# The experts' products in three single passes of numbers in parts, with x held by halves of the tokens

## What is computed

```python
# attention, 16 heads of 32; no scaling of the scores
xq, xk, xv = x @ wq.T, x @ wk.T, x @ wv.T
probs = softmax(einsum('bqhd,bkhd->bhqk', xq, xk))
x = layernorm(x + einsum('bhqk,bkhd->bqhd', probs, xv) @ wo.T)
# experts: E = 8, rank R = 64, one chosen per token
logits = x @ Wr.T + br
expert_weight, expert_idx = max and argmax of softmax(logits)
h = einsum('nd,erd->ner', x, A)
y = einsum('ner,eor->neo', h, B) / 64
x = layernorm(x + y[chosen expert] * expert_weight)
```

## Time and profile before

| | |
|---|---|
| runs | 1540.71 us median of 3 (1540.62 to 1541.03) |
| profiled execution | 1541.77 us, of which 1540.0 us from the first to the last instruction (its span) |
| mean granted clock of PE | 0.986 of full speed |
| busy | PE 1480.7 us (96%), POOL 1159.7 (75%), DVE 932.6 (61%), ACT 776.8 (50%) |
| opening, before slot 0 | 55.9 us |
| slots 0 to 7 | 311.1 us |
| slots 8 and 9 | 43.9 and 45.2 us |
| slots 10 to 14 | 242.6 us |
| slots 15, 16 and 17 | 44.1, 42.4 and 46.3 us |
| slots 18 to 22 | 235.7 us |
| slots 23, 24 and 25 | 44.0, 41.8 and 44.8 us |
| slots 26 to 30 | 205.1 us |
| slot 31 and closing | 33.8 and 103.3 us |
| DMA | 153.13 MB, the queues' packets take 33.5% of the 16 engines' span |

### The profile page before, as it was taken

How to read it: one execution, slowest core, us unless ns; L and a number is a source line. 1 busy time by engine, 2 the same in 40 slices (tenths; PEclk the granted TensorE clock), 3 DMA queues, 4 the chain that set the end, 5 groups by cost and what they waited for, 6 DMA issues and landing times.

```text
span 1540.0 us, 20530 instructions
## 1 busy us (share of the span) xinstructions
PE 1480.7 (96%) x6872; PEld 865.1 (56%) x6872; DVE 932.6 (61%) x1722; ACT 776.8 (50%) x1421; POOL 1159.7 (75%) x654
## 2 busy tenths in 40 slices
PE   7999999989999999999999999999999999999998
PEld 5755456655645656556645555556664555554354
DVE  6756667655565566665566556666556666564633
ACT  3455555544555455545546445554555545455232
POOL 0376879978798867877889987777987888888301
PEclk9999999999999999999999999999999999899999
DMA  7355624444431422427242323324514222210001
GB/s 237 92 165 150 208 80 135 142 148 131 124 77 42 117 84 61 126 80 254 52 130 64 90 70 103 104 68 153 158 39 148 49 49 63 56 42 29 1 13 42
DMA packets 80217, 153.13 MB, mean 99 GB/s; under 512 B 19041, under 2 KB 26225, under 8 KB 79729
## 3 DMA queue, kind: packets, MB, share of 16 engines
q1 hardware_dynamic: 78720, 150.24, 33.5%
q0 software_dynamic: 336, 1.07, 0.2%
q10 hardware_dynamic: 1056, 0.52, 0.1%
HBM read 102.52 MB, written 48.49 MB: 98 GB/s over the span
## 4 chain that ended last, share of the span: by engine, by line
PE 78%; issue 7%; DVE 6%; POOL 4%; DMA 3%; ACT 1%; SPq 1%; POOLq 0%; ACTq 0%; DVEq 0%
PE w L684 14%; PE pv L827 13%; PE mx L805 13%; PE sc L815 13%; PE w L750 6%; PE w L763 6%; PE w L719 5%; DVE mxc L1037 3%; PE mx L778 2%; POOL Psum L595 2%; DMA spread_s<-den_s 1%; PE mx L743 1%; PE mx L763 1%; PE w L727 1%; DMA den_parts<-spread_s 1%
## 5 line engine op out<-in xcount | busy, mean ns | idle before, releaser
L1037 DVE TENSOR_REDUCE mxc<-mx 128x1 f32<-128x512 f32 x1024 | 683.8, 686 | 463.9 <-PE mx L805 460.8
L908 ACT ACTIVATE P<-sc 128x512 f32<-128x512 f32 x1024 | 598.8, 597 | 504.8 <-PE sc L815 490.6
L595 POOL TENSOR_TENSOR Psum<-Psum,P 128x1024 f32<-128x1024 f32 x296 | 695.7, 2383 | 26.5 <-ACT P L908 24.7
L815 PE MATMUL sc<-stack 98*128 98x512 f32 x1024 | 540.4, 530 | 7.5 <-ACT P L908 6.9
L805 PE MATMUL mx<-stack 96*128 96x512 f32 x1024 | 407.1, 402 | 9.1 <-DVE mxc L1037 4.6
L815 PEld LDWEIGHTS sc<-stack 98*128 98x128 f32 x1024 | 194.3, 190 | 142.7 <-issue 81.0
L805 PEld LDWEIGHTS mx<-stack 96*128 96x128 f32 x1024 | 195.9, 191 | 124.2 <-issue 70.8
L827 PE MATMUL pv<-P,V 128*32 128x512 f32 x2048 | 250.4, 607 | 0.0
L592 POOL TENSOR_TENSOR Psum<-P 128x1024 f32<-128x1024 f32 x50 | 118.6, 2390 | 132.7 <-ACT P L908 126.4
L684 PE MATMUL w<-xT_s,wqk_s 128*128 128x512 f32 x624 | 197.9, 408 | 12.0 <-DVE xT_s L1054 10.4
L684 PEld LDWEIGHTS w<-xT_s,wqk_s 128*128 128x128 f32 x624 | 116.9, 192 | 67.7 <-issue 43.4
(11 more groups left out here) (147 smaller groups left out, 1086.8 us busy)
## 6 DMA issues: line engine op xcount, KB each, us to landing
stack<-qk_parts SPq DMA_DIRECT2D x186, 256.0 KB, 4.3
qk_parts<-split SPq DMA_DIRECT2D x56, 512.0 KB, 3.4
wqk_s<-wqk_parts SPq DMA_DIRECT2D x24, 512.0 KB, 4.5
xT_s_f<-xT SPq DMA_DIRECT2D x8, 1024.0 KB, 6.5
den_s<-den_parts SPq DMA_DIRECT2D x124, 64.0 KB, 2.1
r_f<-x SPq DMA_DIRECT2D x3, 2048.0 KB, 11.2
out<-r_f SPq DMA_DIRECT2D x12, 512.0 KB, 3.1
qk_parts<-turned SPq DMA_DIRECT2D x8, 512.0 KB, 3.9
```

What stands on the lines that cost most here:

```text
L595: pool.tensor_tensor(sums(s)[:, i, :], sums(s)[:, i, :], P[:, unit % NP, :], ALU.add).then_inc(add_done, 1)
L815: pe.matmul(sc[c][:, :], stack(s, i)[0:KS, 0, 128 * kb:128 * kb + 128], stack(s, i)[0:KS, 1, 512 * c:512 * c + 512], start=True, stop=True ...
L908: act.activation(P[:, unit % NP, 512 * c:512 * c + 512], sc[c][:, :], ACT.Exp).then_inc(exp_done, 1)
L1037: dve.tensor_reduce(mxc[:, q % 2, at:at + 1], BANK["max", g][:, :], AX.X, ALU.max).then_inc(mx_done, 1)
```

## The change

`h`, `z` and `lg` become three single passes of numbers in parts. What follows from that:

- A, B and Wr are split: A and B in slots 4 and 5 by ACT (high) and POOL (low) in r, and kept in DRAM as `a_parts` and `b_parts` of 2 MB each; Wr in slot 2.
- yT and hmT have a high part by ACT as before and a low part by DVE (`yT_low`, `hmT_low`), read from the transpose's bank, which is now free only after that.
- The experts' parts take place: `wide` holds A's parts (or wv's, as before) and a new `wb` holds B's from slot 9 on. x in parts is held for 512 tokens rather than 1024 (`xT_s`; in batches 0 and 1 the second half lies in `wb`). For batches 2 and 3 the pieces of qk are done for the second half of the tokens first, then for the first half; the parts of the second half are kept in DRAM (`keep_x`) and loaded again for `v` (`again_x`) at the start of slots 16 and 24, whose filler starts at half 8. Each slice of the weights is loaded for each piece.
- P has 6 buffers rather than 7, and slots 4 to 7 leave their last two blocks to PE as slots 0 to 3 do.

```diff
-    NP, NMX = 7, 3
+    NP, NMX = 6, 3
...
-    CHUNKS = {"qk": PASSES * KT, "v": PASSES * KT, "o": KT, "part": KT - 1, "h": KT, "z": KT, "t1": 1, "t2": 1, "lg": 1, "den": 1}
-    COST = {"qk": 13, "v": 13, "t1": 24, "t2": 24}
+    CHUNKS = {"qk": PASSES * KT, "v": PASSES * KT, "o": KT, "part": KT - 1, "h": PASSES * KT, "z": PASSES * KT, "t1": 1, "t2": 1,
+              "lg": 1, "den": 1}
+    COST = {"qk": 13, "v": 13, "h": 13, "z": 13, "t1": 24, "t2": 24}
...
-        some = [len(fill) * (n + 1) // (KB + 2) - len(fill) * n // (KB + 2) for n in range(KB + 2)]
+        some = (2, 2, 2, 1, 1, 0, 1, 2, 1, 1) if fill else (0,) * (KB + 2)
...
+            if not final:
+                FROM[at + PAIRS] = 8
...
+            if batch > 1 and turn == 0:
+                KEEP_X[place + 8] = batch
+        if batch > 1:
+            AGAIN_X[HALVES * PAIRS * batch] = batch
+    SPLIT_AT, WR_AT = {"a": HALVES * 4, "b": HALVES * 5 + 8}, HALVES * 2 + 20
...
     def tail(s):
-        return s < 4 or s == LAST
+        return s < PAIRS or s == LAST
...
+        def x_half(b, c):
+            return (wb_f, wb) if b < 2 and c else (xT_f, xT_s)
...
+            def keep_x(b):
+                sp.wait_ge(x_lo, 2 * KT * b + KT)
+                sp.dma_start(x_d[b - 2], xT_s[:, :, :, :].bitcast(f32)).then_inc(x_kept, 16)
+            def again_x(b):
+                sp.wait_ge(qk_ready, 16 * (b + 1))
+                sp.wait_ge(v_ready, KB * b + KB // 2)
+                sp.dma_start(xT_s[:, :, :, :].bitcast(f32), x_d[b - 2]).then_inc(x_again, 16)
...
-                sp.wait_ge(qk_ready, 4 if j < SLICES + 2 else 2 * (j - 1))
+                sp.wait_ge(qk_ready, 4 if j < SLICES + 2 else last_of(j - 2) + 1)
...
-                for s, d in ((a_s, aT), (b_s, bT)):
-                    sp.dma_start(s, d.rearrange("(k p) n -> p k n", p=128)).then_inc(ab_loaded, 16)
+                sp.dma_start(wide[:, :, :, :].bitcast(f32), a_d).then_inc(a_loaded, 16)
+                if b == 1:
+                    sp.wait_ge(qk_ready, 32)
+                    sp.dma_start(wb[:, :, :, :].bitcast(f32), b_d).then_inc(b_loaded, 16)
...
-                    if n % 2 and n >= 17 and n // 2 + 2 < SLICES * B:
-                        load_weights(n // 2 + 2)
+                    if n >= 16 and n == last_of(load_of(n)) and load_of(n) + 2 < LOADS:
+                        load_weights(load_of(n) + 2)
...
+                for n, place in enumerate(SPLIT_AT.values()):
+                    if half == place - 8:
+                        load_raw_ab(n)
+                    if half == place + 24:
+                        store_ab(n)
...
+                for n, place in enumerate(SPLIT_AT.values()):
+                    if half in range(place + 4, place + 4 + 4 * KT, 4):
+                        ab_low(n, (half - place) // 4 - 1)
...
-                for kt in range(KT):
-                    done = pe.matmul(bank[:, 0:E], yT[:, 128 * kt:128 * kt + 128], wr_s[:, kt, :], start=(kt == 0), stop=(kt == KT - 1))
+                for c in range(PASSES * KT):
+                    kt, at = c // PASSES, slice(128 * (c // PASSES), 128 * (c // PASSES) + 128)
+                    done = one_of_three(bank[:, 0:E], [yT[:, i, at] for i in range(2)], [wr_s[:, i, kt, :] for i in range(2)], c)
...
-                done = pe.matmul(bank[:, :], hmT[:, 128 * kt:128 * kt + 128], b_s[:, kt, :], start=(kt == 0), stop=(kt == KT - 1))
+                done = one_of_three(bank[:, :], [hmT[:, i, at] for i in range(2)], [wb[:, i, kt, :] for i in range(2)], c)
...
-                act.activation(yT[:, :], bank[:, :], ACT.Copy).then_inc(yT_done, 1)
+                act.activation(yT[:, 0, :], bank[:, :], ACT.Copy).then_inc(yT_hi, 1)
...
-                act.activation(hmT[:, :], bank[:, :], ACT.Copy, scale=SCALING).then_inc(hmT_done, 1)
+                act.activation(hmT[:, 0, :], bank[:, :], ACT.Copy, scale=SCALING).then_inc(hmT_hi, 1)
...
+            def yT_low(n, bank):
+                dve.wait_ge(yT_hi, n + 1)
+                dve.tensor_tensor(yT[:, 1, :], bank[:, :], yT[:, 0, :].bitcast(f32), ALU.subtract).then_inc(yT_done, 1)
+            def hmT_low(n, bank):
+                dve.wait_ge(hmT_hi, n + 1)
+                dve.scalar_tensor_tensor(out=hmT[:, 1, :], in0=bank[:, :], scalar=SCALING, in1=hmT[:, 0, :].bitcast(f32),
+                                         op0=ALU.mult, op1=ALU.subtract).then_inc(hmT_done, 1)
...
+                    elif kind == "t1":
+                        yT_low(n, bank)
                     elif kind == "lg":
                         largest_logit(n, bank)
                     elif kind == "h":
                         masked(n, bank)
+                    elif kind == "t2":
+                        hmT_low(n, bank)
```

More of the change, by code:

```diff
@@ L208, in build_attention_lora_moe_block @@
         if half in X_PASS:
-            batch, m = X_PASS[half]
-            frees = next_turn(("xi", 2 * KT * batch + m))
+            batch, turn, kt = X_PASS[half]
+            frees = next_turn(("xi", 2 * KT * batch + KT * turn + kt))
         for kind, n, _ in AT.get(half, ()):
@@ L701, in v @@
                 kt, (b, kb) = c // PASSES, divmod(n, KB)
+                half, at = kb // 4, slice(128 * (kb % 4), 128 * (kb % 4) + 128)
+                x_parts = x_half(b, half)[1]
                 if c == 0:
-                    pe.wait_ge(x_lo, 2 * KT * b + KT * (kb // 4 + 1))
+                    if b > 1 and half:
+                        pe.wait_ge(x_again, 16 * (b - 1))
+                    else:
+                        pe.wait_ge(x_lo, 2 * KT * b + KT * (half + 1 if b < 2 else 2))
                     if b > 1:
@@ L707, in v @@
                     pe.wait_ge(wv_lo, kt + 1)
-                done = one_of_three(bank, [xT_s[:, i, kt, 128 * kb:128 * kb + 128] for i in range(2)],
-                                    [wide[:, i, kt, :] for i in range(2)], c)
+                done = one_of_three(bank[:, :], [x_parts[:, i, kt, at] for i in range(2)], [wide[:, i, kt, :] for i in range(2)], c)
                 if c == PASSES * KT - 1:
@@ L1007, in _ @@
                     x_high(*X_HIGH[half])
+                if half == WR_AT:
+                    act.wait_ge(tail_loaded, 32)
+                    act.activation(wr_s[:, 0, :, :], wr_f[:, 1, :, :], ACT.Copy).then_inc(wr_hi, 1)
+                for n, place in enumerate(SPLIT_AT.values()):
+                    if half in range(place, place + 4 * KT, 4):
+                        ab_high(n, (half - place) // 4)
                 for kind, late in (("o", 7), ("z", 11)):
```

212 lines of the change are left out of this document (127 added, 85 removed).

## The result

The changed kernel takes 1638.06 us (median of 4 runs, 1633.08 to 1642.49), the kernel before 1540.87 beside it: a ratio of 1.062, 95% interval 1.058 to 1.066. The forecast was 1551 with a range up to 1567, so the time lies 71 us outside. The sign was the one held likelier; the size was not even near. The profiled execution took 1638.73 us, its span 1636.9.

A forecast was written before the change was run, and what follows sets the result against it. PE, busy 96% of the span, was taken as the bound, with POOL setting slot 7. Terms -4.3 - 13.0 + 14.4 + 4.3 - 6.3 + 5.5 + 3.6 + 6 = +10.2 on 1540.7 gave 1551; own range 1543 to 1560, whole range 1526 to 1567.

The forecast's parts named there:

- The sign: Whole kernel: slower held at 0.55, faster 0.33, same 0.12; said to be decided at 0.6 us for each of 18 places.
- PE, in order, waits 1.3 ... I count 12 such places ... at 1.2 us: +14.4: Slots 10 to 14 and 18 to 22: hmT_low on DVE frees t2's bank late, so PE waits; +14.4 us.
- its twin for slots 26 to 30: Slots 26 to 30: hmT_low delays lg and the maximum, PE waits at six places at 1.8 us; +10.8.
- nothing, as long as that cover stays: After t1: yT_low's later release of the bank costs nothing, the third bank being wanted three halves later with a product between.
- The splits on ACT ... and the opening: nothing: Copies to DRAM, ACT's splits (8 x 0.6) and the opening cost nothing, lying under PE's work.
- I take this 13.3 as gone: Slot 7: its 13.3 us over slot 5 vanish as slots 4 to 7 lose two POOL adds each.
- the splits, forecast at 3.5: Slots 4 to 8: splitting A and B costs 3 us at the dens of slots 4 and 5, 0.5 for a store.
- 3 x 0.7: Closing: the extra VectorE step on yT and hmT is uncovered at the first two and last tile, +2.2 us.
- slot 9: Slot 9: 2.1 MB more of A's and B's parts ahead of the denominators' small transfers makes DVE's reciprocal wait, +5.5 us.
- the waits in slots 15 and 23: The third qk piece needs its own weight slice, which comes 1.8 us late in each slot: +3.6.
- The products' 19.5: Slots 10 to 14, 18 to 22 and 26 to 30: cheaper pieces less dearer lg save 13.0 and 6.5 us.
- the ring does not bind: Rival: DVE is early enough at t2, so the 14.4 and 10.8 vanish; 1526 us, faster; chance 0.2.

The follow-up runs named there:

- hold_in_before: The kernel before, with only the transposes' banks in the loop of slots held until a VectorE subtraction nobody reads: 1595.37 us, ratio 1.034.
- no_low: The changed kernel without yT_low and hmT_low, ScalarE's copy freeing the bank and the high part passed again: 1576.76 us, 1.022 to the kernel before.
- four_moves: The changed kernel with x's second load, Wr's split, A's and B's low parts, and the loads of their parts put elsewhere: 1618.51 us, 1.050 to before.
- low_unread: The changed kernel with both low parts made and freeing the bank, but products and logits reading the high part twice: 1632.17 us, 1.059 to before.

## Why the prediction was wrong

**The step that failed first** is "PE, in order, waits 1.3 ... I count 12 such places ... at 1.2 us: +14.4", with its twin for slots 26 to 30 at 1.8. It prices a wait as its own length and puts the clock after it at nothing. hold_in_before shows the whole of this step by itself: 58.3 us where the forecast had 14.4 + 10.8 = 25.2. The waits were nearly right (PE's waits rose by 26.0); missing was half clock, another 34.

In the changed kernel it is the same. For hmT PE waits 15 times, 1.25 us on the average, in slots 10 to 14 and 18 to 22 (forecast 12 at 1.2), and 6 times, 1.5 on the average, in slots 26 to 30 (forecast 6 at 1.8). The waits for yT, which the forecast put at "nothing, as long as that cover stays", come to 7.4 us more. All waits of PE in the expert slots rise by 31.3 us (14.2 to 45.5). Half clock in them grew by 75.1 us, of which half, 37.5, is lost; less the 19.3 that the products gain by no_low, the three make 49.5, against 50.7 measured. The rows for it were there: the profile before had 41 us at half clock, mostly behind its few waits.

**VectorE beside GpSimd.** "The splits on ACT ... and the opening: nothing" has no term for Wr's low part on DVE. It cost 12 us (slot 2: 35.6 before, 47.7 after, 35.8 once it was moved). The reason shown: both its operands are in SBUF, and it did not get done beside GpSimd's additions; the same subtraction, moved to where GpSimd is idle, takes 0.18 us. The Trainium skill, SBUF — State Buffer, "Who interferes with whom", states it: "A DVE instruction with two SBUF inputs contends with a GpSimd instruction that reads SBUF". The trace agrees, 11.19 us beside additions against 0.18 beside none. The same section of the Trainium skill counts copies among what can take the shared port, and the copy's 11.17 agrees too. The kernel before hinted at it: it passes batch 1's x through PSUM (`xi`) before DVE subtracts.

**The first batch.** "I take this 13.3 as gone" takes all by which slot 7 is longer than slot 5 for what the removal of its wait brings. Alone, with the passes for the dens, the change gave 5.4 in the trace, where the forecast had 9.8, and nothing by the medians. And the splits, forecast at 3.5, cost 12.9. With them the den of slot 6 waits 6.1 behind POOL, whose additions have four low parts of 1.3 us among them there, and slot 5's first score product waits 4.8 for a stack's rows, which were asked for at 263.03, 4.0 us behind the 2 MB store of A's parts (8.0 us to landing). Half clock follows both.

**The opening** was put at nothing and cost 3.4: both halves of x are asked for at once, ahead of the weights' rows. Restoring the wait of the second half for the first took it back (55.7 in four_moves).

**The closing.** The pieces came out as priced (2.88 and 1.25). But the forecast put the low part's latency at 3 x 0.7, and low_unread shows 8.9. Without the low parts (no_low) slot 31 and the closing are 8.7 shorter than before, so this latency eats all that the products gain.

**Right:** the price of a pass and of lg; slot 9 (+7.2 against 5.5, and moving A's and B's loads took it back); the waits in slots 15 and 23 (2.1 and 2.3) and 16 and 24, +10.2 against 9.6 together; the shorter ring of P at nothing. The products' 19.5 in the expert slots come out once no_low's extra waits and half clock are counted (19.3). The rival "the ring does not bind" fell outright. The sign came out as held likelier; the clock, the largest single part of the miss, stood in no rival either. Two slips of the sum change nothing: 3 x 0.7 is 2.1, not 2.2, and by the forecast's own terms the sign turns at 0.8 us for each of the 18 places (15.0 of waits), not at 0.6.

## What to carry to other kernels

A wait on a saturated TensorE costs its length and, in this kernel, on the average somewhat more than as much again at half clock (26 and 34 us in hold_in_before); price both, above all where it repeats. Before moving the release of a shared PSUM bank to another engine, list what stands ahead of the release on that engine. And look at every new VectorE instruction, however small, for two SBUF operands or a copy beside a busy GpSimd.

## What the runs showed of the hardware

- DVE's 128x32 subtraction and even a copy of 16 columns lasted in slot 2 until the end of POOL's unbroken run of additions (11.2 us, across the ends of four of them), but in slot 3 got in after the end of one (2.2 us). The Trainium skill, SBUF — State Buffer, "SBUF: two separate sides", tells of a wait for the instruction that holds the shared port, which fits the 2.2 us and not the 11.2; what lets GpSimd's next addition go first in one place and not in the other stays open. A maximum over one SBUF operand took 0.16 us beside additions.
- Half clock came in stretches of 3.4 us or a multiple. Six planted waits of 0.7 to 0.8 us left full clock alone; in all traces half clock followed waits over 2.5 us 66 times of 69 and those of 0.7 to 2.5 us about two times in five. So a price for each wait can only be given on the average.
- Twelve single passes with new weights each over 8 columns took 1.25 us, 0.104 a pass, no less than the 0.101 of an FP32 record. The four records of the transpose behind them, over 128 columns, stand 0.10 apart (1578.40 to 1578.81), so from 8 to 128 columns the spacing does not go with the columns; at 512 it is 0.24 (2.88 us for twelve).
